# Layer 1's first norms, mod rows and weight halves inside layer 0's FFN, and inverse roots by Newton steps on VectorE

## The reference

```python
mod = (_silu(L1_c) @ L1_wmod).reshape(L1_c.shape[0], 6, 1, -1)
sa, ca, ga, sb, cb, gb = (mod[:, 0], mod[:, 1], ...)
ga = (2 * (ga >= 0) - 1) * jnp.maximum(jnp.abs(ga), 0.25)
h = _layernorm(x, axis=-1) * (1 + ca) + sa
x = x + ga * _L1_attn_ref(h, ...)
h = _layernorm(x, axis=-1) * (1 + cb) + sb
x = x + gb * _L1_ffn_ref(h, ...)
```

## Time and profile before

| what | value |
|---|---|
| median of 3 runs | 777.65 us (776.88 to 778.69) |
| profiled execution | 778.5 us, its span 776.7 us |
| PE, weight loads (PEld) | busy 721.5 us (93%), 620.7 us (80%) |
| DVE, ACT, POOL | busy 556.8 us (72%), 447.5 us (58%), 372.5 us (48%) |
| HBM | 18.01 MB read, 1.05 MB written |

### The profile page before, as it was taken

The page is one execution under the profiler, slowest core; times in us unless marked ns, Lnnn a source line. Parts: engine busy times, 40 slices in busy tenths (PEclk is TensorE's granted clock), DMA queues, the critical chain, the costliest instruction groups (busy, mean ns, idle before and its releaser), DMA issues. The chain is left out here.

```text
span 776.7 us, 12379 instructions
## 1 busy us (share of the span) xinstructions
PE 721.5 (93%) x4376; PEld 620.7 (80%) x4376; DVE 556.8 (72%) x1263; ACT 447.5 (58%) x924; POOL 372.5 (48%) x403
## 2 busy tenths in 40 slices
PE   6979989999999999999999799999979999789997
PEld 4858878888888888888888689997768778577787
DVE  4656786678766787767776788776579788566666
ACT  2756656667566676666655343322578776546432
POOL 2685556635766357653451330002756545205773
PEclk8999999999999999999999999999999999999999
DMA  7000000000000000004000040004100000000001
GB/s 250 14 8 8 8 22 15 14 2 14 22 15 8 8 15 14 14 8 170 7 8 8 9 128 1 1 1 126 39 0 2 1 1 1 0 4 0 1 1 55
DMA packets 19115, 19.85 MB, mean 26 GB/s; under 512 B 2158, under 2 KB 17006, under 8 KB 19054
## 3 DMA queue, kind: packets, MB, share of 16 engines
q1 hardware_dynamic: 17934, 18.40, 7.3%
q10 hardware_dynamic: 1120, 0.66, 0.3%
HBM read 18.01 MB, written 1.05 MB: 25 GB/s over the span
## 5 line engine op out<-in xcount | busy, mean ns | idle before, releaser
L633 ACT ACTIVATE at_probs<-at_probs,at_negmax 128x128 f32<-128x128 f32 (+7 forms) x128 | 99.6, 778 | 31.8 <-DVE at_negmax L736 29.7
L935 POOL TENSOR_TENSOR at_swapped<-at_swapped,at_sin 128x512 f32<-128x512 f32 x40 | 52.1, 1302 | 136.0 <-ACT at_swapped L611 136.0
L736 DVE CUSTOM_DVE_ANT_0 at_probs<-at_scores,causal 128x128 f32<-128x128 f32 (+7 forms) x128 | 96.1, 751 | 16.8 <-PE at_scores L59 16.2
L524 PE MATMUL at_turn<-ident_sb,at_probs 128*128 128x128 f32 x576 | 85.0, 274 | 13.2 <-DVE at_full_T_lo L752 11.1
L524 PEld LDWEIGHTS at_turn<-ident_sb,at_probs 128*128 128x128 f32 x576 | 66.5, 140 | 21.8 <-issue 8.4
L626 ACT ACTIVATE at_edge_T_hi<-at_turn 128x128 fp32r<-128x128 f32 (+3 forms) x128 | 55.5, 434 | 33.2 <-PE at_turn L524 32.8
L57 PE MATMUL at_scores<-at_kT_hi,room 128*128 128x512 f32 (+1 forms) x192 | 66.4, 346 | 3.4 <-DVE at_negmax L736 3.4
L626 ACT ACTIVATE at_full_T_hi<-at_turn 128x512 fp32r<-128x512 f32 x64 | 38.3, 598 | 49.5 <-PE at_turn L524 47.4
L58 PE MATMUL at_scores<-at_kT_lo,room 128*128 128x512 f32 (+1 forms) x192 | 66.7, 347 | 0.0
L59 PE MATMUL at_scores<-at_kT_hi,room 128*128 128x512 f32 (+1 forms) x192 | 66.3, 345 | 0.0
L752 DVE TENSOR_TENSOR at_edge_T_lo<-at_turn,at_edge_T_hi 128x128 fp32r<-128x128 f32 (+3 forms) x128 | 61.3, 479 | 1.1 <-ACT at_edge_T_hi L626 0.8
(11 more groups left out here) (405 smaller groups left out, 2292.3 us busy)
## 6 DMA issues: line engine op xcount, KB each, us to landing
at_wq_in<-L_attn_Wqkv SPq DMA_DIRECT2D x16, 128.0 KB, 2.2
at_wo_in<-L_attn_Wo SPq DMA_DIRECT2D x16, 128.0 KB, 2.0
staging<-L_ffn_routed_w SPq DMA_DIRECT2D x7, 256.0 KB, 4.8
ff_wmod<-L_wmod SPq DMA_DIRECT2D x1, 1536.0 KB, 6.2
at_wmod<-L_wmod SPq DMA_DIRECT2D x1, 1024.0 KB, 8.6
staging<-L_ffn_w_gate SPq DMA_DIRECT2D x1, 1024.0 KB, 5.2
staging<-L_ffn_w_up SPq DMA_DIRECT2D x1, 1024.0 KB, 7.3
staging<-L_ffn_w_down SPq DMA_DIRECT2D x1, 1024.0 KB, 9.7
```

The lines of the kernel that those rows point to most:

```text
L524: mm = pe.transpose(p_turn[t % 2][:, b - b0, :], probs[:, s % 4, b * P:(b + 1) * P], m.ident[:, :])
L633: act.activation(row, row, ACT.Exp, scale=-1.0, bias=negmax[:, unit % 4:unit % 4 + 1], accum_out=rowsum[:, unit // NT % 2, i:i + 1])\
L736: dve.tensor_tensor_reduce(out=probs[:, s % 4, 0:width], in0=p_scores[s % 2][:, 0:width], in1=m.causal[:, S - width:], scale=-1.0, scalar= ...
L935: turning = pool.tensor_tensor(swapped[:, r % 2, :], swapped[:, r % 2, :], sin[:, cols], ALU.mult)
```

## The change

Four things change.

- inverse_roots no longer needs a root from ACT: one operation adds eps, one makes a first guess on the integer bits, and three Newton steps of three operations follow, eleven chained operations on DVE. The table loads for Sqrt and Sigmoid between the stages go with it or move.
- The rows part of layer 1's modulation weights (1 MB) is loaded in attention0 into the space of its first keys, and PE makes the modulation rows at ffn0's start, where keep_warm's 7 and 9 matmuls were (2 remain). The columns part is loaded at ffn0's start and multiplied before its last two down products.
- Inside ffn0's units now lie: the high halves of wq, wv and wk (ACT, unit 1) and their low halves (POOL), the bounding of both gate rows, wo's product with the gate and its halves (POOL), small weights (DVE, unit 1), and both norms of tiles 0 to 3, with the transposes between down of unit 5 and the up product of unit 7. The first norm of tiles 4 and 5 ends ffn0 on DVE.
- attention1 is one Block. Four jobs (early_jobs) use the columns of tiles 0 to 3 while DVE and ACT make the norms of tiles 6 and 7 and the second norm of tiles 4 to 7; the transposes of those follow and then the last jobs before the slots. The key job of the second head's first columns is no longer in a slot. There is no keep_warm in it, and no wait for wo. Late holds the buffers that both stages share.

```diff
-def inverse_roots(dve, m, chain, tiles, n):
...
-    dve.wait_ge(m.sqrt_out, n)
-    chain.run(dve.reciprocal(rstd, root))
-    chain.run(dve.tensor_tensor(rough, rstd, rstd, ALU.mult))
-    chain.run(dve.tensor_tensor(rough, rough, vareps, ALU.mult))
-    chain.run(dve.tensor_scalar(rough, rough, -0.5, 1.5, ALU.mult, ALU.add))
-    chain.run(dve.tensor_tensor(rstd, rstd, rough, ALU.mult))
...
+    rough, rstd, vareps, var = m.tiny[:, 1, cols], m.rstd[:, cols], m.vareps[:, cols], m.meanvar[:, cols, 1]
+    as_int = mybir.dt.int32
+    chain.run(dve.tensor_scalar(vareps, var, EPS, None, ALU.add))
+    chain.run(dve.tensor_scalar(rstd.bitcast(as_int), vareps.bitcast(as_int), -0.5, float(0x5F3759DF), ALU.mult, ALU.add))
+    for _ in range(3):
+        chain.run(dve.scalar_tensor_tensor(out=rough, in0=rstd, scalar=-0.5, in1=vareps, op0=ALU.mult, op1=ALU.mult))
+        chain.run(dve.tensor_tensor(rough, rough, rstd, ALU.mult))
+        chain.run(dve.scalar_tensor_tensor(out=rstd, in0=rough, scalar=1.5, in1=rstd, op0=ALU.add, op1=ALU.mult))
...
+                def turn_g():
+
+                    pe.wait_ge(h32_done, CHUNKS)
+                    pe.wait_ge(g_done, 4)
+                    for k in range(KD):
+                        for n in FIRST_TILES:
+                            mm = pe.transpose(p_g[k][:, n * P:(n + 1) * P], g_row[:, n, k * P:(k + 1) * P], m.ident[:, :])
+                        mm.then_inc(g_mm, 1)
+
+                pe.wait_ge(m.mod_in, 32)
+                mod_rows(0)
                 turn_x(0)
                 turn_x(1)
-                keep_warm(pe, idle_bank, m.room, 9)
+                mod_rows(1)
+                keep_warm(pe, p_gate[:, 0:2, :].rearrange("p e t -> p (e t)"), m.room, 2)
...
-                    if 2 <= u < UNITS - 1:
+                    if u >= 2:
                         down(u - 2)
+                    if u == 7:
+                        turn_g()
...
-                down(UNITS - 3)
-                mod_rows(0)
-                mod_rows(1)
                 mod_columns()
...
+                def normalize(c):
+                    act.wait_ge(rstd_done, c + 1)
+                    for n in (2 * c, 2 * c + 1):
+                        act.activation(late.h_row[:, n, :], m.x[:, n, :], ACT.Identity, scale=m.rstd[:, n:n + 1], bias=m.nbias[:, n:n + 1]).then_inc(h_normed, 1)
...
                 for u in range(UNITS):
                     silu(u)
+                    if u == 0:
+                        read_rows()
+                    if u == 1:
+                        attention_weights_hi()
                     if u in (2, 4):
                         scale_shift(u // 2 + 1)
+                    if u == 4:
+                        normalize(0)
+                    if u == 5:
+                        mean_squares(0)
+                    if u == 6:
+                        normalize(1)
+                        mean_squares(1)
+                        roots()
+                        load_table(act, m, ACT.Silu, 0)
+                    if u == 7:
+                        turned_hi()
                     magnitude(u)
-                read_rows()
-                read_gates()
+                load_table(act, m, ACT.Sqrt, 0)
+                read_columns()
...
+                def row_roots(c):
+                    tiles = (2 * c, 2 * c + 1)
+                    stats(c)
+                    variances(dve, m, chain, tiles)
+                    inverse_roots(dve, m, chain, tiles)
+                    spread(dve, m, tiles).then_inc(rstd_done, 1)
...
+                inverse_roots(dve, m, chain, LAST_TILES)
                 low_x(1)
-                inverse_roots(dve, m, chain, LAST_TILES, 4)
                 norm(LAST_TILES)
                 for u in range(UNITS):
                     c, half = divmod(u, 2)
                     multiply(u)
-                    if u >= 3 and half and u < UNITS - 1:
+                    if u in (3, 5):
                         add(c - 1)
-                    if u == UNITS - 1:
-                        add(CHUNKS - 2)
+                    if u == 5:
+                        row_roots(1)
+                    if u == 6:
+                        inverses()
+                    if u == 7:
+                        stats(2)
+                        variances(dve, m, chain, (4, 5))
                     sparsify(u)
-                    if u >= 3 and half and u < UNITS - 1:
-                        stats(c - 1)
-                stats(CHUNKS - 2)
-                add(CHUNKS - 1)
-                stats(CHUNKS - 1)
+                    if u == 1:
+                        small_weights()
+                    if u == 3:
+                        row_roots(0)
+                    if u == 6:
+                        add(2)
+                inverse_roots(dve, m, chain, (4, 5))
+                for n in (4, 5):
+                    chain.step(dve.scalar_tensor_tensor(out=late.h_row[:, n, :], in0=m.x[:, n, :], scalar=m.meanvar[:, n, 0:1], in1=m.mod_row[:, 1, :],
+                                                        op0=ALU.subtract, op1=ALU.mult))
+                chain.settle()
+                for n in (4, 5):
+                    dve.scalar_tensor_tensor(out=late.h_row[:, n, :], in0=late.h_row[:, n, :], scalar=m.rstd[:, n:n + 1], in1=m.mod_row[:, 0, :],
+                                             op0=ALU.mult, op1=ALU.add)
...
+                def mod_rows(c):
+                    for n in (2 * c, 2 * c + 1):
+                        rows = late.h_row[:, n, :]
+                        pool.wait_ge(h_normed, n + 1)
+                        pool.tensor_tensor(rows, rows, m.mod_row[:, 1, :], ALU.mult).then_inc(h_done, 1)
+                        pool.wait_ge(h_done, 2 * n + 1)
+                        pool.tensor_tensor(rows, rows, m.mod_row[:, 0, :], ALU.add).then_inc(h_done, 1)
+
                 pool.wait_ge(m.staged, 48)
                 pool.wait_ge(wu_ready, KD)
                 for c in range(I0 // P):
                     rows = wd_in[:, c * DM:(c + 1) * DM]
                     pool.tensor_tensor(rows, rows, m.gate[:, 0, 1, :], ALU.mult).then_inc(wd_ready, 1)
-
-                for c in (2, 3):
-                    pool.wait_ge(hx_hi, c + 1)
-                    pool.tensor_tensor(m.hT.lo[:, :, chunk_cols(c)], h32[c % 2][:, :, :], as_f32(m.hT.hi[:, :, chunk_cols(c)]), ALU.subtract)\
-                        .then_inc(hx_ready, 1)
-
-
-def attention1(nc, a, m, sems, sb, split):
+                pool.wait_ge(mod_read, 3)
+                bounded_gate(0)
+                pool.wait_ge(w_hi, 2)
+                pool.tensor_tensor(late.wq.lo, late.wq_in, as_f32(late.wq.hi), ALU.subtract)
+                pool.tensor_tensor(late.wv.lo, late.wv_in, as_f32(late.wv.hi), ALU.subtract)
+                low_x(2)
+                pool.wait_ge(w_hi, 4)
+                pool.wait_ge(up_mm, 3)
+                for n in range(2):
+                    pool.tensor_tensor(late.wk.lo[:, :, :, n, :], late.wk_in.rearrange("p k (g d) -> p k g d", d=D1),
+                                       as_f32(late.wk.hi[:, :, :, n, :]), ALU.subtract)
+                pool.wait_ge(up_mm, 4)
+                pool.wait_ge(m.staged1, 80)
+                for n in range(H1):
+                    chain.step(pool.tensor_tensor(late.wo_in[:, n, :], late.wo_in[:, n, :], m.gate[:, 1, 0, :], ALU.mult))
+                low_x(3)
+                chain.settle()
+                chain.run(pool.tensor_scalar(late.wo.hi, late.wo_in, 1.0, 1.0, ALU.mult, ALU.mult))
+                mod_rows(0)
+                pool.wait_ge(up_mm, 6)
+                chain.step(pool.tensor_tensor(late.wo.lo, late.wo_in, as_f32(late.wo.hi), ALU.subtract))
+                mod_rows(1)
+                pool.wait_ge(late.inverted, 1)
+                for n in FIRST_TILES:
+                    pool.tensor_scalar(g_row[:, n, :], late.h_row[:, n, :], late.inv[:, n:n + 1], 1.0, ALU.mult, ALU.mult).then_inc(g_done, 1)
+                for k in range(KD):
+                    pool.wait_ge(g_hi, k + 1)
+                    pool.tensor_tensor(m.hT.lo[:, k, 0:BANK], g32[:, k, :], as_f32(m.hT.hi[:, k, 0:BANK]), ALU.subtract)
+                bounded_gate(1)
...
-                    keep_warm(pe, idle_bank[:, :], m.room, 50)
...
-                    keep_warm(pe, idle_bank[:, :], m.room, 12)
...
+        early_jobs = [("k", 0, 0), ("qq", 0, 0), ("v", 0, 0), ("k", 1, 0)]
+        jobs = early_jobs + [("k", 0, 1), ("qq", 0, 1)]
+        first = [p_scores[1][:, 0:BANK], p_scores[1][:, BANK:S]]
+        first += [p_turn[n][:, :, :].rearrange("p a b -> p (a b)") for n in range(2)] + [p_proj[:, :], p_att[:, :]]
+        jobs += [("v", 0, 1), ("k", 1, 1), ("q", 2, 0), ("q", 2, 1), ("q", 3, 0), ("q", 3, 1)]
+        first_slot = dict(zip(jobs[6:], (1, 5, 10, 13, 17, 19)))
...
-                for n, job in jobs_of(-1):
+                for n, job in enumerate(early_jobs):
+                    project(n, *job)
+                turn_g()
```

(17 more changed lines are left out.)

432 lines of the change are left out of this document (202 added, 230 removed).

## The result

The changed kernel takes 782.02 us (median of 4 runs, 781.91 to 783.04), the kernel before 777.40 in the same comparison: ratio 1.0055, 95% interval 1.004 to 1.0071. The forecast was 782.3.

What follows compares the result with a forecast made beforehand. It took PE to bound the FFN before and DVE's two-norm chain the head, with DVE the later engine in the changed units. FFN +2.3 + 14, head -14.1, tails +2.5 sum to +4.7 us: 782.3, range 772.5 to 788.

Steps and rivals of the forecast that it cites:

- Sum: Whole kernel: FFN's end, head and tails together give +4.7 us, so 783.2 profiled and 782.3 as median.
- Start, +5.7: Layer 0's FFN start: longer root chains, partly beside POOL, move the first product from 458.69 to about 464.4.
- Pace and additions, 57.7 + 12.2: FFN units: DVE, the later engine, takes 8 x 7.21 = 57.7 us, plus 12.2 of added DVE work.
- Contention, c = 14: FFN units: about 26.2 us of new POOL work lengthens DVE's operations by 14 us, bounds 0 and 17.7.
- The FFN's end, +16.3: Layer 0's FFN ends 2.3 + c later than 532.32, which is 16.3 us with c = 14.
- The head, -14.1: Layer 1's attention, start to fifth slot's scores: 24.5 us in place of 38.6, with 16.9 to the first scores.
- The tails, +2.5: End of attention 1 and start of FFN 1: each waits for six more operations, +1.25 us each.
- rival 3: FFN units: all of POOL's time is lost, c = 17.7, 786.1 us, or 787.8 with PE's lower clock; chance 0.15.
- Rival 1: Units 1 to 6: POOL misses DVE, c below 9.3, faster, 770.1 us at c = 0; chance 0.27.
- Rival 2: Gains and losses cancel: c between 8 and 11, time within 1.55 us of 777.65; chance 0.13.
- Rival 4: Head: early jobs wait for the tiles' low halves from POOL, starting it 2.6 us late; no chance of its own.
- The signs: FFN's last product near 548, DVE busy above 0.9 of units, line 1281's four above 2 us, head some 24.5.

Runs made afterwards that it cites:

- tail_fill: Changed kernel with 17 in place of 12 fill matmuls ahead of the last transposes of layer 1's attention: 781.36 us.
- gates_wo_back: Changed kernel with POOL's bounding of both gate rows and wo's product and split moved back to the start of layer 1's attention: 780.94 us.
- pool_more: Changed kernel with wo's low half computed four times in place of once on POOL: 789.69 us.
- window: Changed kernel with POOL's pieces in the FFN's units each held until DVE has ended the mask of the unit before: 779.51 us.
- the best version: Changed kernel with old roots where ACT's table allows, POOL's work windowed, four scaled rows on ACT, second gate in slots: 765.76 us; one window mended, 763.99.

## Why the prediction was right, point by point

- *Sum.* 782.3 against 782.02, and the mechanism holds: DVE became the bound in the units, and POOL's work lengthened its operations. But the terms are off in both directions: by the places of the two profiles they come to 2.9 where 4.7 was worked out, and the profiled execution took 781.92, not 783.2. That the medians differ by 4.6 all the same is luck; 1.7 of the other 1.8 us come from the execution of before that was profiled and from time outside the span.
- *Start, +5.7.* Measured +2.8. The step that failed: six more operations of 0.70 under POOL and a longer norm behind them. The chain of tiles 4 to 7 took 2.9 more, not 4.2, since POOL's gate bounding followed its eight products, and under its first operation DVE's small ones took 0.16 to 0.33. The four norm operations took 0.5 less, not 0.3 more (2.11 against 2.62). The chain of tiles 0 to 3 took 1.0 more, as worked out (1.2), but it began 0.6 earlier, at 443.95 in place of 444.53, which the prediction didn't have.
- *Pace and additions, 57.7 + 12.2.* Held: 2.33 us from the product to the mask and 4.88 for it. By the rows the additions inside the units are 7.6, where the prediction has 8.3, so the two counts of c, 12.5 and 13.3, are one. Those behind the units took 4.0 where it has 3.9.
- *Contention, c = 14.* Measured 12.5 to 13.3. The share of 0.72 was too small for an operation that hits (2.13 of 2.55), and too large for those that fell on the product or a wait.
- *The FFN's end, +16.3.* Measured +12.7. The start is 2.9 smaller and c some 1 us; PE's last down product at the lower clock added 0.6: DVE was done at 544.0, PE at 544.6. The sum of the prediction also adds the 0.3 us by which, in its words, PE ends earlier.
- *The head, -14.1.* Measured -13.4 to the fifth scores. The chain to the first scores took 14.4 us where 16.9 was worked out. Up to the transposes it fits (9.1 against 9.4), but these and the high and low halves were added one behind the other, 4.1 us, and they overlap: the first matmul of k's second half begins 2.2 after the first transpose. From the first scores to the fifth it took 10.8 in place of 7.6, and 10.26 before. Neither wo's wait nor the key job was worth its time in the slots: with them gone PE waits 1.97 for ACT's exponentials.
- *The tails, +2.5.* Measured +3.9: 1.1 and 1.2 as worked out, and 1.6 by PE's clock in fill matmuls that end a Block. The prediction had the clock only in rival 3, for the head, where this execution had 1.00 up to the first scores and those of tail_fill, gates_wo_back, pool_more and window had not.
- *Rival 1* (POOL misses DVE) was wrong for this kernel and right as a possibility: in the best version most of POOL's pieces miss DVE, and it is 1.7% faster than before. *Rival 3's* full lock is what a hit does; it isn't what the whole of POOL's work does. *Rival 2* needed c from 8 to 11, which 12.5 to 13.3 isn't. *Rival 4* didn't occur: the low halves of the first tiles were made by 532.4, long before the early jobs.
- *The signs.* The last product ends at 544.6, not near 548; DVE is busy for 0.897 of the units, just under the 0.9; the four of line 1281 take 2.54 where POOL runs, PE's waits in the units are put down to DVE (all but 0.65 us), and from the Block's start to the fifth scores it is 25.2 us, not 24.5.

## What to carry to other kernels

Before work is moved to an idle engine, look at which operations of the bound engine it will stop, and begin it at a moment when that engine does something that can't be stopped: in the changed kernel the same POOL work lengthened DVE's operations by 13.3 us begun when its inputs were ready, and by 7.3 begun at the end of DVE's mask. That is worth only what the next bound leaves: 2.5 us of time here, and some 7 in the best version, where PE waited less for POOL. A chain of tiny dependent operations cost 0.2 us each where it stood on the path, so a root from an idle engine with its table loaded beat three Newton steps. And price the parts of a change apart: here the roots alone lost 11.4 us in the kernel before, more than the whole change, and with most of them taken back the rest was 2.8 us faster than before.
